# A four-layer graph network kernel: in the first edge stage two products become one of 128 rows, with a window of 63 target rows

## What is computed

```python
# 3125 nodes; 100000 edges, sorted by dst
dst = minimum((3125 * uniform(100000) ** 2.0).astype(int32), 99999)   # then argsort(dst)
# layer 0
mi  = concatenate([x[src], x[tgt], edge_attr_64], 1)        # both directions of each edge
h   = relu(layernorm(mi @ msg_w1 + msg_b1) * g + b) @ msg_w2 + msg_b2
agg = segment_sum(h, tgt, 3125)
# layer 1 also wants, per node, the largest and the sum of exp of edge_weight over edges of one src
```

## Time and profile before

| | us |
|---|---|
| median of 3 runs | 5465.92 |
| lowest and highest | 5465.03, 5468.97 |
| the profiled execution, its own time | 5450.14 |
| its span in the trace | 5448.2 |
| first edge stage: first and last addition of `dve_t` (L1078) start at | 86.6 and 2397.4 |
| first edge stage: last scatter (L1405) starts at | 2454.5 |

### The profile page before, as it was taken

One profiled execution on the slowest core, in us unless ns is written; L12 is line 12 of the kernel. 1 busy time (PEld: TensorE's weight loads), 2 busy tenths in 40 slices (PEclk: granted clock), 3 DMA queues, 4 the chain that ended last, 5 costly groups with the idle time before them and its releaser, 6 DMA issues.

```text
span 5448.2 us, 94725 instructions
## 1 busy us (share of the span) xinstructions
PE 4679.2 (86%) x27130; PEld 3397.1 (62%) x27130; DVE 4596.6 (84%) x13376; ACT 3625.1 (67%) x12260; POOL 4070.7 (75%) x3716
## 2 busy tenths in 40 slices
PE   4899999999999999985888889588888886999995
PEld 3777777777777777765555555355555554455553
DVE  5999999999999999986888888688888877777776
ACT  4777777777777777762777777367777763555553
POOL 4788888888888888884777777577777764777776
PEclk7889999989899999997999989699999998999998
DMA  6867777777666666653777777467666762555553
GB/s 221 159 158 177 181 181 176 181 177 176 161 158 155 161 157 156 160 105 96 195 202 197 202 196 197 139 210 215 210 212 208 212 188 84 160 156 161 156 161 110
DMA packets 636916, 935.13 MB, mean 172 GB/s; under 512 B 105224, under 2 KB 346114, under 8 KB 635730
## 3 DMA queue, kind: packets, MB, share of 16 engines
q1 hardware_dynamic: 416690, 580.51, 34.4%
q0 software_dynamic: 219680, 348.31, 30.5%
HBM read 613.49 MB, written 314.95 MB: 170 GB/s over the span
## 4 chain that ended last, share of the span: by engine, by line
POOL 50%; issue 20%; PE 14%; DVE 8%; DMA 5%; ACT 2%; POOLq 0%; DVEq 0%; SPq 0%; ACTq 0%
POOL arena L1787 27%; POOL tab L1405 12%; POOL arena L1429 10%; DMA tab<-arena 3%; DMA arena<-T,srcI 2%; PE PS L2313 2%; PE PS L1974 2%; PE PS L2291 1%; PE PS L809 1%; PE PS L1018 1%; PE PS L1749 1%; PE PS L1020 1%; PE PS L1028 1%; PE PS L2303 1%; PE PS L1040 1%
## 5 line engine op out<-in xcount | busy, mean ns | idle before, releaser
L1787 POOL DMA_INDIRECT arena<-T,srcI x2112 | 2018.4, 956 | 797.8 <-issue 629.6
L1405 POOL DMA_INDIRECT tab<-arena x680 | 1117.4, 1643 | 230.7 <-issue 209.4
L1429 POOL DMA_INDIRECT arena<-T,srcI x784 | 800.6, 1021 | 270.7 <-issue 231.6
L1774 DVE TENSOR_TENSOR_SCAN arena<-arena,PS 128x512 f32<-128x512 bf16 x588 | 748.3, 1273 | 169.6 <-PE PS L2625 81.1
L1758 ACT ACTIVATE arena<-PS 128x512 f32<-128x512 f32 x588 | 347.9, 592 | 616.5 <-PE PS L1749 616.5
L1854 DVE TENSOR_SCALAR arena<-PS,nodeid 128x512 bf16<-128x512 f32 x908 | 627.1, 737 | 76.2 <-PE PS L1835 76.2
L2607 PE MATMUL PS<-arena 128*128 128x512 bf16 x2400 | 555.4, 382 | 0.0
L1974 PE MATMUL PS<-arena 128*128 128x396 bf16 x2800 | 540.0, 350 | 8.4 <-DVE arena L1854 7.2
L1018 PE MATMUL PS<-We,arena 65*128 65x256 f32 x1568 | 493.3, 397 | 62.2 <-DVE arena L1078 50.1
L809 PE MATMUL PS<-arena 128*128 128x448 bf16 x2184 | 535.1, 404 | 0.8 <-DVE arena L824 0.8
L1365 ACT ACTIVATE arena<-arena 128x128 bf16<-128x128 f32 x1568 | 459.5, 300 | 39.5 <-DVE arena L1078 39.5
(11 more groups left out here) (321 smaller groups left out, 10958.2 us busy)
## 6 DMA issues: line engine op xcount, KB each, us to landing
H<-arena SPq DMA_DIRECT2D x784, 256.0 KB, 2.4
arena<-keepR SPq DMA_DIRECT2D x294, 256.0 KB, 4.7
arena<-wF SPq DMA_DIRECT2D x98, 512.0 KB, 5.5
arena<-T,srcI POOLq DMA_INDIRECT x2896, 3.4
arena<-in_ea64T SPq DMA_DIRECT2D x98, 256.0 KB
arena<-sH SPq DMA_DIRECT2D x98, 256.0 KB
arena<-dH SPq DMA_DIRECT2D x98, 256.0 KB
arena<-S SPq DMA_DIRECT2D x98, 256.0 KB
```

Of the source, the lines that this page charges most:

```text
L1405: e.indirect_dma_start(out=tabs[k % KT], out_offset=at_rows(iA[b % 10][:, c:c + 1]), in_=X2[n % 3][:, c, :], in_offset=None, compute_op=AL ...
L1429: e.indirect_dma_start(out=Gs[b % NR][:, c, :], out_offset=None, in_=T0, in_offset=at_rows(srcI[:, CB * b + c:CB * b + c + 1])).then_inc(g ...
L1774: ins = e.tensor_tensor_scan(s[b % n][:, h, :], kR[g % 6][:, h0:h0 + CB * P], src[h], s[(b - 1) % n][:, h, CB * P - 1:CB * P] if b else in ...
L1787: e.indirect_dma_start(out=dst[:, c, :], out_offset=None, in_=T_tab, in_offset=at_rows(srcI[:, CB * b + c:CB * b + c + 1])).then_inc(gs.of ...
```

## The change

One window now has 63 rows (`WIN`), and edge features, window and bias share the 128 rows of one product: rows 0 to 63 of `eT` are the edge features, rows 64 to 126 the one-hot of the target, and row 127 is one. `Wt` holds the weights, the 63 rows of `T0` and the bias in the same rows. The marks for edges outside the window use `WIN` too. DVE makes `OL`, the one-hot `eq` of the high bits, and `RH` of a pair by one instruction each. PE places every fifth batch (36 of them), and its 14 steps per two batches are spread over 20 half iterations.

```diff
+WIN = 63
@@ edge_lists
-                e.dma_start(We[64:65, 0:P], A["L0_gnn_msg_b1"]...
+                e.wait_ge(s_const, 1)
+                e.dma_start(We[127:128, 0:P], A["L0_gnn_msg_b1"]...
-                e.tensor_scalar(out_w, rel, float(P), None, ALU.is_ge).then_inc(own.sem, own.up())
+                e.tensor_scalar(out_w, rel, float(WIN), None, ALU.is_ge).then_inc(own.sem, own.up())
-                e.tensor_scalar(wcol[:, :], d0B, small[:, 12, 0:1], -float(MID), ALU.add, ALU.add)
+                e.tensor_scalar(wcol[:, :], d0B, small[:, 12, 0:1], cols[:, 7:8], ALU.add, ALU.mult)
@@ Spread
+                self.turns = [4 * M * k // 14 for k in range(14)]
-                self.hot = arena.get(CB, NBLK)
-            def at(self, i):
-                s, u = divmod(i - self.first, 2 * self.M)
-                return (s, u) if 0 <= s < self.n // 2 and u < 14 else (None, None)
+            def at(self, t):
+                s, u = divmod(t - 2 * self.first, 4 * self.M)
+                if not 0 <= s < self.n // 2 or u not in self.turns:
+                    return None, None
+                return s, self.turns.index(u)
@@ L0_edges
-            pk = Spread(7, 26)
+            pk = Spread(5, 36)
-            Tw = [arena.get(2 * P) for _ in range(2)]
-            OT = [arena.get(CB * P) for _ in range(2)]
+            Wt = [arena.get(2 * P) for _ in range(2)]
+            eq = arena.get(C2, NBLK)
-                e.dma_start(dR[g % 2], grow(dH, g)).then_inc(ld_d.of(g), 16)
+                e.dma_start(dR[g % 2][64:P, :], dH[g * GE:(g + 1) * GE].rearrange("(a n) -> a n", a=1).to_broadcast([64, GE])
+                            ).then_inc(ld_d.of(g), 16)
+                if g < 2:
+                    e.wait_ge(s_wt, 1)
-                e.dma_start(Tw[g % 2][:, 0:P], T0[bass.ds(v, P), P:2 * P]).then_inc(ld_t.of(g), 16)
-                e.dma_start(Tw[g % 2][:, P:2 * P], T0[bass.ds(v, P), 0:P]).then_inc(ld_t.of(g), 16)
+                e.dma_start(Wt[g % 2][64:64 + WIN, 0:P], T0[bass.ds(v, WIN), P:2 * P]).then_inc(ld_t.of(g), 16)
+                e.dma_start(Wt[g % 2][64:64 + WIN, P:2 * P], T0[bass.ds(v, WIN), 0:P]).then_inc(ld_t.of(g), 16)
@@ pe_C
-                    e.matmul(psC[:, c * 2 * P:(c + 1) * 2 * P], eT[g % 2][0:65, h0 + c * P:h0 + (c + 1) * P],
-                             We[0:65, :], start=True, stop=False)
-                    ins = e.matmul(psC[:, c * 2 * P:(c + 1) * 2 * P], OT[b % 2][:, c * P:(c + 1) * P], Tw[g % 2],
-                                   start=False, stop=True)
+                    ins = e.matmul(psC[:, c * 2 * P:(c + 1) * 2 * P], eT[g % 2][:, h0 + c * P:h0 + (c + 1) * P], Wt[g % 2],
+                                   start=True, stop=True)
@@ dve_A
-                for c in range(C2):
-                    k = C2 * g + c
-                    e.tensor_scalar(OL[:, c, :], iotaf[:, :], loF[:, k:k + 1], None, ALU.is_equal)
+                e.tensor_tensor(eq, bc(iotaf[:, 0:NBLK], C2), bf(hiF[:, C2 * g:C2 * g + C2], NBLK), ALU.is_equal)
+                e.tensor_tensor(OL, bc(iotaf[:, :], C2), bf(loF[:, C2 * g:C2 * g + C2], P), ALU.is_equal)
-                for c in range(C2):
-                    k = C2 * g + c
-                    ins = e.scalar_tensor_tensor(out=RH[:, c, :, :], in0=bc(iotaf[:, 0:NBLK], 2), scalar=hiF[:, k:k + 1],
-                                                 in1=bf(first[:, c, :], NBLK), op0=ALU.is_equal, op1=ALU.mult)
+                ins = e.tensor_tensor(RH, eq.unsqueeze(2).to_broadcast([P, C2, 2, NBLK]),
+                                      first.unsqueeze(3).to_broadcast([P, C2, 2, NBLK]), ALU.mult)
@@ dve_OT
+                if b >= 4:
+                    e.wait_ge(C.of(0), C.at(b - 4))
-                e.tensor_scalar(OT[b % 2], dR[g % 2][:, h0:h0 + CB * P], wcol[:, g:g + 1], None, ALU.is_equal
-                                ).then_inc(OTd.of(0), 1)
+                e.tensor_scalar(eT[g % 2][64:P, h0:h0 + CB * P], dR[g % 2][64:P, h0:h0 + CB * P], cols[64:P, 7:8],
+                                wcol[64:P, g:g + 1], ALU.mult, ALU.is_equal).then_inc(OTd.of(0), 1)
```

More of the change, by code:

```diff
@@ L778, in dve_count, with dve_onehot @@
                     e.tensor_tensor(outc[:, :], outc[:, :], self.psN, ALU.add)
-            def dve_onehot(self, e, i):
-                s, v = divmod(i + 1 - self.first, 2 * self.M)
-                if not 0 <= s < self.n // 2 or v >= 14 or v % 4 >= 2:
+            def dve_onehot(self, e, t):
+                s, v = self.at(t + 1)
+                if s is None or v % 4 >= 2:
                     return
@@ L812, in pe_step, with dve_flush @@
                 ins.then_inc(self.step.of(0), 1)
-            def dve_flush(self, e, i, accT, zeroed):
-                s, v = divmod(i - 2 - self.first, 2 * self.M)
-                if not 0 <= s < self.n // 2 or v % 2 or v >= 14:
+            def dve_flush(self, e, t, accT, zeroed):
+                s, v = self.at(t - 1)
+                if s is None or v % 2 == 0:
                     return
@@ L1064, in pe @@
                         pe_B(e, i - 7)
+                    pk.pe_step(e, 2 * i)
                     if 0 <= i - 2 < NBAT:
```

47 lines of the change are left out of this document (24 added, 23 removed).

## The result

| | us |
|---|---|
| before, median of 4 runs | 5465.99 (5465.03 to 5468.97) |
| after, median of 4 runs | 9387.22 (9384.96 to 9389.15) |
| ratio, with its 95% interval | 1.7172 (1.7142 to 1.7202) |
| predicted | 9073, between 8100 and 9750 |

The account below looks back on a forecast made before the run. POOL was taken to bound the first edge stage. 5450.1 us (the profiled execution) - 78 for fewer scatters + 3685 for the branch (196 x 18.8) = 9057; with 15.8 to the median, 9073 us, range 8100 to 9750.

Parts of the forecast that it names:

- What bounds the stage: First edge stage: POOL's queue is never empty, so POOL bounds it, although PE and DVE are busy for 94%.
- The branch taken in all batches: POOL, all 196 batches: one mark anywhere, padding included, sends every batch through the never-taken branch with eight adding indirect DMAs.
- Wait for the gathers and restart, 1.95 us: POOL in the branch, per batch: waiting until its own last gather lands, 1.75 us, and starting again, about 0.2 us.
- Adds at 1.54 with a gap of 0.30: POOL in the branch: eight adding gathers, seven before the last at 1.84 us each, 12.9 us a batch.
- The rival with cheap adds: Adds in the branch cost 0.94 us like plain gathers, not 1.54: 941 us less, 8130 us; chance 25%.
- Landing of the last, 4.0 us: End of the branch, per batch: the last add's data arrives 4.0 us after issue, between crowded 5.37 and quiet 3.18 to 3.66.
- the rival with dear landings: Branch landings at crowded values (2.45 and 5.37 us), 1.88 an add: 21.2 us a batch, 9540 us in all; chance 20%.
- The gap before the next item exists already: POOL after the branch's last landing: the usual gap before the next item is no new cost, so nothing was added.
- 40 scatters fewer, 78 us: POOL, first edge stage: ten batches fewer to scatter, 40 x (1.643 + 0.31), save 78 us, and this gain stays.
- DVE and PE worth nothing: First edge stage: net 25 us less on DVE and some 280 us less on PE count for nothing beside POOL.
- the rival where the branch is not taken: Marks come out at zero; POOL stays the bound with 40 scatters fewer: 5388 us, faster by 1.4%; chance 2%.
- The other stages unchanged: Sign to look for in the profile: everything outside the first edge stage stays as it was.

Follow-up runs that it names:

- the plain gathers: The kernel after with the eight DMAs of the branch as plain gathers into a spare tile, without the add: 8475.38 us, ratio 1.5518.

## Why the prediction was right, and where it was off

Point by point, against the steps of the prediction.

- **What bounds the stage: right.** POOL's work and waits account for the whole of the 3934 us to 0.2 us, and the other engines idle.
- **The branch taken in all batches: right**, 1568 and 392 instructions, and the kernel before with a threshold of 118 shows that marks alone do it. Without marks the time is 5436 us.
- **Wait for the gathers and restart, 1.95 us: too low.** 2.10 in the batch shown. Over all batches it is 2.41, the idle time before L1426 and the two small operations that run inside the wait, (394.8 + 77.1) / 196; some waits were far longer, as the last number (the longest) of this row says:

```profile
POOL arena L1426 <- DMA arena<-T,srcI: 394.8, 192, 14.0
```

- **Adds at 1.54 with a gap of 0.30: right.** 1.556 measured, and the plain gathers showed that the add is what is paid for. The rival with cheap adds falls by this. It priced the difference at 941 us, and the plain gathers measured 912.
- **Landing of the last, 4.0 us: too low.** 4.1 to 4.7 in the detours looked at, 4.3 on the average by POOL's idle time behind the eighth add (3.76 + 1.55 - 0.98). The rows it rested on the earlier trace rows were scatters to many rows. I had named the repeated row in the rival with dear landings and given it no number of its own; it was 1.0 us a batch. The rival itself was half right: its wait for the gathers, 2.45, is what the average shows, its landing of 5.37 is a microsecond too dear, and its 9540 lies nearer to the measured time than 9073 does. The time alone would not have chosen the forecast over it; the landings did.
- **"The gap before the next item exists already": too low.** After the landing POOL needs 0.98 us until the next DMA starts (the chain above: L1418, L1430, 0.73 of issue), 0.68 more than a gap. The prediction has no term for leaving the branch.

Together: 2.41 + 13.0 + 4.3 + 0.68 = 20.4 us, and (3934.2 + 78) / 196 = 20.5 by the stage's end, where the prediction had 18.8. The missing 1.7 us, 196 times, are 330 us, and the forecast was 314 too low. The mechanism was right; two terms were sized short and one was missing, all in the same direction, so the forecast held because its range was wide enough for them.

- **40 scatters fewer, 78 us: right where POOL is alone.** Between the kernel before with a threshold of 118 and the kernel after lie 77 us by the medians. "It stays", on the bound, held only while the detour kept the other engines idle.
- **DVE and PE worth nothing: right for this kernel, wrong as the prediction used it in the rival where the branch is not taken.** There it said 5388, since "DVE and PE keep up". Measured 5436. DVE did not lose the 25 us (2202.8 us against 2201.9), at 94% it was as good as a second bound (32 us of new waits for ACT), and POOL's own instructions lengthened (40 us), in part at least by an edit on DVE, which the prediction did not consider at all.
- **A small count is off.** The rows add up to 1228 waits and not 1222; nothing hangs on it.
- **The other stages unchanged: right**, 2999 against 2994 us.

## What to carry to other kernels

A flag that is computed from data and guards slow work for all tiles is part of a change of any size or threshold that feeds it: work out its value, with the padding, before costing the edits that the diff shows. Cost a serial detour by all its parts, from the last thing it waits for to the first instruction behind it, and ask what its idle lanes read. Where the next engine is at 94%, do not count on the whole gain of relieving the first: here 25 of 78 us arrived.

## What the runs showed of the hardware

- An indirect DMA of 128 rows took 0.94 to 0.97 us of POOL's time without an add (gathers into the arena, L1787 and the plain gathers in the branch) and 1.54 to 1.56 with one, both into the arena (1556 ns) and to memory. In the busy part of the stage both were longer on the average, 1021 and 1643 ns.
- For the same bytes, 128 rows of 512 bytes, the gather with an add made 144 packets and the plain one 32.
- 128 rows fetched with an add landed 4.1 to 4.7 us after the start when all 128 were the same row, and 3.1 to 3.9 us when they were 128 different ones (13 and 20 detours from 3000 us on).
- Coming out of a branch that ended in a wait for a DMA cost POOL 0.98 us to the start of its next DMA, against the 0.30 us between two DMAs in a row.
- A POOL scatter that started beside a `tensor_tensor` of 128 x 1024 with both inputs in SBUF took longer by what was left of it, 2.47 and 2.69 us instead of 1.58 in the two shown, in 22 of 22 cases. In the four kernels with `OL` by eight `tensor_scalar` and the merged product, two of them with a two-input instruction of 128 x 400, 0 to 3 of over 1060 DMAs were long.
